# A chain of graph and expert layers on one core: the attention stage's order of work, and the number of weight buffers in two expert stages

## What is computed

```python
# L1: a shared gated layer, plus for each token its experts' second matrices
# L2: eight transformer experts, two chosen per token; keys and values of ALL tokens
def _expert(x, ...):
    q, k, v = to_heads(x @ Wqkv.T + bqkv)                 # 8 heads of 32
    attn = softmax(q * scale @ k.T)                        # over all 1354 tokens
    x = layernorm(x + (attn @ v) @ Wo.T + bo)
    h = gelu(x @ W1.T + bf1)                               # 256 -> 1024
    h = gelu(h @ W2.T + bf2)                               # 1024 -> 256
    return layernorm(x + h)
# L3: eight experts, two chosen per token
    y = layernorm(relu(x @ W1 + b1) @ W2 + b2) * gamma + beta
```

## Time and profile before

| what | value |
|---|---|
| median of 3 runs | 3437.53 us (3427.68 to 3438.13) |
| the profiled execution | 3433.94 us, its span 3432.2 us |
| routed tiles of L1 (first turned rows to last product) | 1275.7 to 1360 us of the span |
| attention stage (first to last turned unit) | 1716.8 to 2850.5 us |
| last expert stage (first weights issued to last result) | 3121.1 to 3397.8 us |
| busy, of the span | PE 73%, PE weight loads 61%, DVE 48%, ACT 32%, POOL 15% |
| mean granted TensorE clock | 0.852 |

### The profile page before, as it was taken

One profiled execution on the slowest core, in us unless ns is written; L12 is line 12 of the kernel. 1 busy time (PEld: TensorE's weight loads), 2 busy tenths in 40 slices (PEclk: granted clock), 3 DMA queues, 4 the chain that ended last, 5 costly groups with the idle time before them and its releaser, 6 DMA issues. The chain is left out here.

```text
span 3432.2 us, 53128 instructions
## 1 busy us (share of the span) xinstructions
PE 2519.3 (73%) x18781; PEld 2109.8 (61%) x18781; DVE 1643.4 (48%) x3169; ACT 1102.1 (32%) x2154; POOL 522.7 (15%) x805
## 2 busy tenths in 40 slices
PE   6978698599676687549688888888888885433334
PEld 4867597599466356438567777777777774333323
DVE  3646322322366311334377777777777774333113
ACT  2333121122133111012155555555555552231100
POOL 0000122122121015000001111111111112002112
PEclk9999699699798799769899999999999997666655
DMA  4000122243310027216634114424444201202231
GB/s 114 1 7 1 55 86 86 68 134 98 90 65 25 25 101 250 49 35 247 245 97 109 58 35 115 117 63 108 130 115 131 77 23 38 50 1 96 89 98 64
DMA packets 145018, 291.44 MB, mean 85 GB/s; under 512 B 36146, under 2 KB 73048, under 8 KB 141684
## 3 DMA queue, kind: packets, MB, share of 16 engines
q1 hardware_dynamic: 124532, 231.40, 21.9%
q0 software_dynamic: 20224, 56.65, 6.1%
HBM read 496.49 MB, written 65.74 MB: 164 GB/s over the span
## 5 line engine op out<-in xcount | busy, mean ns | idle before, releaser
L2215 PE MATMUL tx_ring<-g_ident,tx_p 128*128 128x128 f32 x2552 | 427.3, 299 | 128.6 <-issue 45.4
L2215 PEld LDWEIGHTS tx_ring<-g_ident,tx_p 128*128 128x128 f32 x2552 | 315.5, 151 | 222.9 <-issue 63.6
L2434 DVE TENSOR_REDUCE tx_neg_max<-tx_scores 128x1 f32<-128x1354 f32 x232 | 362.2, 1561 | 28.1 <-PE tx_scores L2203 28.1
L2441 DVE COPY tx_p_t<-tx_ring 128x512 f32<-128x512 f32 x464 | 306.9, 687 | 135.5 <-PE tx_ring L2215 130.1
L2341 ACT ACTIVATE tx_p<-tx_scores,tx_neg_max 128x1354 f32<-128x1354 f32 x232 | 322.3, 1389 | 77.1 <-DVE tx_neg_max L2434 76.8
L2203 PE MATMUL tx_scores<-tx_keys,tx_queries 96*128 96x512 f32 (+1 forms) x696 | 222.4, 432 | 13.7 <-DMA tx_queries<-tx_q_hi 11.3
L2348 ACT ACTIVATE tx_p_t<-tx_ring 128x384 f32<-128x384 f32 x232 | 113.4, 489 | 357.8 <-PE tx_ring L2215 356.7
L2753 PE MATMUL nee_wide<-nee_xg_t,nee_w 128*128 128x128 f32 x232 | 55.3, 414 | 156.6 <-issue 156.6
L2254 PE MATMUL tx_ring<-tx_p_t,tx_values 128*32 128x128 f32 x5104 | 151.3, 274 | 21.2 <-ACT tx_p_t L2348 20.8
L2254 PEld LDWEIGHTS tx_ring<-tx_p_t,tx_values 128*32 128x32 f32 x5104 | 135.8, 110 | 34.7 <-ACT tx_p_t L2348 34.0
L2753 PEld LDWEIGHTS nee_wide<-nee_xg_t,nee_w 128*128 128x128 f32 x232 | 48.2, 308 | 165.3 <-issue 165.3
(11 more groups left out here) (907 smaller groups left out, 5430.6 us busy)
## 6 DMA issues: line engine op xcount, KB each, us to landing
tx_keys<-expert_keys SPq DMA_DIRECT2D x696, 169.5 KB
lv1e_w<-in_L_ffn_W SPq DMA_DIRECT2D x232, 256.0 KB
tx_w<-in_L_ffn_W SPq DMA_DIRECT2D x58, 1024.0 KB
lv0e_w<-in_L_ffn_W SPq DMA_DIRECT2D x200, 256.0 KB
tx_values<-expert_values SPq DMA_DIRECT2D x58, 704.0 KB
tx_rows<-in_L_ffn_rows SPq DMA_DIRECT2D x29, 640.0 KB, 3.7
g_adj_t<-in_adj_t POOLq DMA_DIRECT2D x4, 3872.0 KB, 23.1
sro_we<-_L_ffn_expert_out_weight SPq DMA_DIRECT2D x29, 512.0 KB
```

What stands on the lines that cost most here:

```text
L2215: last = nc.tensor.transpose(ring[u % 2][:, (t - t0) * P:(t - t0 + 1) * P], p[n % 2][:, t * P:(t + 1) * P], g.ident[:])
L2434: nc.vector.tensor_reduce(neg_max[:, n % 4:n % 4 + 1], sc[n % 2][:, 0:N], AX_X, ALU.max, negate=True)\
L2441: nc.vector.tensor_copy(p_t[:, n % TURNED, t0:t0 + nt, :], ring[u % 2][:, 0:nt * P].rearrange("p (t q) -> p t q", q=P))\
```

## The change

1. Both weight rings get deeper: `ROUTED_SETS` 3 to 5, `SETS` 3 to 6. A load is then skipped only if the tile five (six) earlier had the same expert.
2. In every head PE's order becomes `turn 0, scores (head + 2), turn 1, turn 2`.
3. `second` moves from head 7 to head 6, on PE and in the ring; `add_second` moves on DVE from the end of head 7 to head 6.
4. `output` is copied out of PSUM by ACT (`keep_output`, at head 1 ahead of `keep_rows`); DVE then adds the residual in SBUF.
5. `split_queries` moves from DVE (head 2) to POOL, behind `middle_rows` and ahead of `fetch`.
6. `mix` waits for unit 2's copy only before its third group of blocks.

```diff
-ROUTED_SETS = 3
+ROUTED_SETS = 5
...
-             5: ("first0", "first1"), 7: ("second",)}
+             5: ("first0", "first1"), 6: ("second",)}
...
-                  "values0": "dve", "values1": "dve", "output": "dve", "second": "dve"}
+                  "values0": "dve", "values1": "dve", "output": "act", "second": "dve"}
...
-                for c in (1, 2):
-                    written(pe, at["heads", i, (4 * half + 3, c)])
+                written(pe, at["heads", i, (4 * half + 3, 1)])
                 for t in range(NB):
+                    if t == TG[2][0]:
+                        written(pe, at["heads", i, (4 * half + 3, 2)])
...
                         turn(i, hd, 0)
-                        turn(i, hd, 1)
                         if HEADS * i + hd + AHEAD < heads:
                             scores(HEADS * i + hd + AHEAD)
+                        turn(i, hd, 1)
                         turn(i, hd, 2)
...
-                    if hd == 7 and i:
+                    if hd == 6 and i:
                         second(i - 1)
...
+            def keep_output(i):
+                u = at["output", i, 0]
+                act.wait_ge(full, u + 1)
+                if i:
+                    act.wait_ge(x1_n_done, i)
+                nc.scalar.activation(x1[:], ring[u % 2][:, 0:D], ACT.Copy).then_inc(drained["act"], 1)
...
             def middle_stats(i):
-                u = at["output", i, 0]
-                dve.wait_ge(full, u + 1)
+                written(dve, at["output", i, 0])
                 dve.wait_ge(residual, i + 1)
-                nc.vector.tensor_tensor(x1[:], ring[u % 2][:, 0:D], x_res[:, i % 2, :], ALU.add).then_inc(drained["dve"], 1)
-                written(dve, u)
+                link(nc.vector.tensor_tensor(x1[:], x1[:], x_res[:, i % 2, :], ALU.add))
...
+            def split_queries(i):
+                written(pool, at["queries", i, 0])
+                pool.wait_ge(q_done, i + 1)
+                if i:
+                    pool.wait_ge(q_stacked, 16 * 12 * i)
+                own(nc.gpsimd.tensor_copy(q_hi[:], q[:]))
+                nc.gpsimd.tensor_tensor(q_lo[:], q[:], q_hi[:], ALU.subtract).then_inc(q_split, 1)
...
                     inverse_std(i - 1, 0, x1_seen, std1_done)
                     middle_rows(i - 1)
+                if i + 1 < tiles:
+                    split_queries(i + 1)
                 if i + 2 < tiles:
                     fetch(i + 2)
...
-SETS = 3
+SETS = 6
```

More of the change, by code:

```diff
@@ L2410, in _ @@
                         keep_inverse(i - 1, 1)
-                    if hd == 1 and i + 1 < tiles:
-                        keep_rows(i + 1)
+                    if hd == 1:
+                        if 0 < i <= tiles:
+                            keep_output(i - 1)
+                        if i + 1 < tiles:
+                            keep_rows(i + 1)
                     if hd == 2 and i + 1 < tiles:
@@ L2449, in scale_bias @@
                     .then_inc(q_scaled, 1)
[L2451 to L2457, removed]
             def inverse(i, half):
@@ L2525, in _ @@
             scale_bias(0)
-            split_queries(0)
             row_max(0)
@@ L2545, in _ @@
                             middle_norm(i - 1)
-                        if i + 1 < tiles:
-                            split_queries(i + 1)
                     if hd == 3 and i < tiles:
@@ L2551, in _ @@
                         context(i, 0)
-                    if hd == 6 and i >= 2:
-                        end_stats(i - 2)
+                    if hd == 6:
+                        if i >= 2:
+                            end_stats(i - 2)
+                        if 0 < i <= tiles:
+                            add_second(i - 1)
                     if hd == 7:
@@ L2558, in _ @@
                             inverse(i, 1)
-                        if 0 < i <= tiles:
-                            add_second(i - 1)
             back.mix(dve, spare)
@@ L2612, in _ @@
                 fetch(i)
+            split_queries(0)
             for i in range(tiles + 2):
```

## The result

The changed kernel takes 3246.3 us (median of four runs, 3244.91 to 3248.6); the kernel before took 3435.57 us (median) beside it. The ratio is 0.9453 [0.9436, 0.947]. The forecast was 3242 us. The profiled execution has a span of 3242.7 us, 189.5 us less than before's 3432.2. Where those went is read from the windows.

A forecast was written before the change was run, and what follows sets the result against it. The last expert stage was held bound by a closed chain over three weight sets, the attention stage by PE; 3434 - 165 - 30 = 3239, for the median 3242 us, range 3180 to 3325.

The forecast's parts named there:

- Part 1: Last expert stage: SETS 3 to 6 lets weight loads run ahead, paced by DMA; -165 us.
- The closed chain: Last expert stage: with three sets product, DVE, SP and transfer follow without overlap, about 11 us a round.
- I take 3.45 us, the DMA's: Last expert stage: the new pace per tile is the DMA's, 1025 KB at 297 KB per us.
- Part 2: Routed tiles: ROUTED_SETS 3 to 5 removes a 2.3 us wait, costs four more real loads; taken as 0.
- Part 3: Attention stage: waits removed, -91 us, against +63 us for the new order; taken as -30 us.
- "issue", 43.3 us: Attention stage, head 7: PE's wait for the exponent is filled by the moved `second`; all 43.3 us gone.
- the `mix` waited for unit 2's copy anyway: Attention stage, heads 0 and 4: the new order adds no wait there, so only six heads pay.
- 0.36 us more per head: Attention stage: PE idles for unit 1's bank in the new order, six heads by 29 tiles, +63 us.
- DVE `tx_p_t`, 32.5 us: Attention stage, head 3: unit 2's wait for copies behind `split_queries` goes with the split off DVE; all gone.
- The 0.36 us is larger: Rival, attention stage: all eight heads pay, port contention adds 32 us, clock falls; 3325 us, chance 0.15.
- Clock returns: Rival, attention stage: without the gap at head 7 PE runs warm; -57 us more, 3185, chance 0.2.
- The slower rival: Split on POOL becomes the bound; its pair must take 11.7 us to lose the gain; chance 0.02.

The follow-up runs named there:

- e1: The kernel before with SETS = 6 alone; 3262.97 us, ratio 0.9504.
- e5: The changed kernel with SETS = 4 instead of 6; 3298.13 us in one run.
- e10: The changed kernel with the last stage's second broadcast row not loaded after the first six tiles, same four issues per tile; 3240.63 us in one run.
- e11: e9 with a last-stage tile's two weight matrices in one buffer, loaded by one DMA, three issues instead of four; 3151.45 us, ratio 0.918.
- e12: e3 with `second` on PE and `add_second` on DVE back at head 7; 3201.96 us, ratio 0.9335.
- e3: The changed kernel with each head back to turn 0, turn 1, scores, turn 2; 3206.46 us, ratio 0.9339.
- e7: The changed kernel with DVE's two inverses between its copies of units 0 and 1 at heads 3 and 7, `end_norm` at head 6; 3191.39 us, ratio 0.9294.
- e4: The changed kernel with `split_queries` back on DVE at head 2; 3307.09 us, 61 us more than the changed kernel.
- e2: The changed kernel with both counts of weight sets back at 3, so the attention edits alone; 3425.54 us, ratio 0.9981.
- e9: The changed kernel with e7's two DVE moves and unit 1 back before the scores; 3167.15 us, ratio 0.9227.

## Why the prediction held, and which of its steps failed

**Part 1, -165 us: right in cause, short by 10, and wrong in what paces.** Measured -174.9 in the trace, -170 for e1 alone. The closed chain is shown by e5's pairs of loads. The step that failed is "I take 3.45 us, the DMA's". Its number came out, 3.46 us in the mean of 20 rounds, but the DMA engines do not set it: with an eighth of the bytes left out (e10) it was 3.49. SP's issue sets 3.2 us of it, and pauses of SP that no run explains make the rest. That the two sums agree is luck. The 10 us lie elsewhere: the first six loads, which wait for nothing, start within 13.9 us where the sum had 17.3; from the start of the 26th load to the last result it is 18.7 us instead of 22.8; and 3 us were given away in taking 165 for 168. The stage counted from its first issue is 101.8 us instead of 3230 - 3121 = 109. The step that set aside the page's rate argued from 311 GB/s. The 312 GB/s of the window above agree with it, but e10 shows that the rate did not matter. The Trainium skill ("DMA: Bandwidth & Descriptors", section on the anatomy of one DMA) has the 436 GB/s as a fit for transfers that GpSimd issues. It gave 7 us less than I took, because by it SP paces; SP does, but for another reason, and the densest 60 us read here, e11's, moved 321 GB/s. The rival "PE paces" fell: clock 0.94 in the dense part, as taken, against 0.62 over the stage before. The 26 real loads were as counted: the first skipped issue is the one at 3192.51 us.

**Part 2, 0: within the error.** The matrix wait of 2.3 us is gone, and the wait for result buffers is 2.5 us longer. No run has this edit alone.

**Part 3, -30 us: the sign right, the account wrong in four places.**

- *"issue", 43.3 us, "All gone".* The row vanished, the time did not: e12 against e3 is 4.5 us less without the edit, within the scatter. I had read what PE waits for at head 7 and named nothing that is late next. The next was DVE's queue from head 7 to head 0.
- *Head 0: "the `mix` waited for unit 2's copy anyway".* True for unit 2's copy, but unit 2 itself now waits 1.56 us for the copy of unit 0, because `row_max` comes later by the scores and DVE's `end_norm` and `inverse` stand behind it, ahead of that copy. This is the missing term; e7 prices it, with head 4's share and the clock, at 55 us.
- *"0.36 us more per head", +63 us.* The extra waits are 0.46 us. Head 1 takes 2222.38 - 2219.89 = 2.49 us from its start to the extra, where it was 2.04: 0.45 us more. As an estimate from this one head, 0.45 x 6 x 29 = 78 us; head 2's wait is shorter, 0.24 us.
- *DVE `tx_p_t`, 32.5 us, gone, and clock 0.* The split on POOL was worth 61 us in whole times and 52 us in the attention stage (e4), 15 of waits and 31 of PE's busy time among them. I had put the clock at zero between -57 and +57; it gave back 18 us of PE's busy time in the change as made.

Two terms were better than forecast: ACT `tx_h` kept 5.5 of 22.2 us where I left 14, and the wait for the bank of `output` fell from 12.6 us to 6.9 with ACT's copy, where I gained 0. That copy and the split wait of `mix` were never undone alone.

So -91 + 63 became, in the runs: about -61 for the split with its clock, about 0 for `second`, +40 for the order of the units; -21, against the 9.5 us of the trace and the 7.5 us of e2. (These prices come from different neighbours and need not add up.) That the total came out 4 us from the forecast is luck: Part 1 gave 10 us more and Part 3 some 20 us less, and 5 us came from outside both.

**The rivals.** "The 0.36 us is larger" was half right: the 0.36 was 0.45, some 15 us more by the estimate above, but the clock rose where the rival had it fall. "Clock returns" named the right price and the wrong place: the gap at head 7 went and the clock rose from 0.95 to 0.97 only, for a gap of the same length opened at head 0. With both closed (e7, e9) the clock is 1.00 and PE's busy time is 42 us below before's. The Trainium skill ("TensorE: Matmul & The Clock Gate", Part 4) says that transposes do not count as busy as matmuls do, which I took as speaking against this rival; the runs speak the other way, since e9's attention stage holds 1.00 with 396 of PE's 940 busy us in transposes (L2215). The slower rival was far off: the two POOL operations are

```profile
L2594 POOL CAST tx_q_hi<-tx_q x29: 393/398/401, 1698.2 to 2779.3; 128x256 fp32r<-128x256 f32 x29
```

```profile
L2595 POOL TENSOR_TENSOR tx_q_lo<-tx_q,tx_q_hi x29: 723/729/733, 1698.7 to 2779.8; 128x256 fp32r<-128x256 f32 x29
```

1.13 us together for the 1.5 forecast and the 11.7 that the rival needed, and the scores never had to wait for them after the first tile.

## What to carry to other kernels

A wait that is removed from one engine is time that another engine used to catch up; before it is booked as gain, add up the other engine's queue over the stretch and name what is late next, and move that work in the same edit (here worth 39 to 55 us). When a closed chain over k buffers bounds a loop, its period divided by the tiles that it serves gives the number of buffers at which the next resource takes over; here that was the issuing queue and not the bytes, though the DMA engines were 97% busy. A change of several edits can be right in sum and wrong in its parts: undoing them one at a time found one that cost 40 us and one worth nothing. And where one stage scatters by 11 us between traces of the same code, a difference of whole times below that is read stage by stage.

## What the runs showed of the hardware

**PE's longer waits and its clock.** Waits of 1.29 to 1.64 us once per tile or more (head 7 before and in e12, head 3 in e4, head 0 in after and e3) go with stage clocks of 0.95 to 0.98, and in e4 the scores behind one take 1.48 us for 0.86, most of them at 1.2 GHz. Not every such wait is followed by a slow stretch: behind the 1.56 us wait shown for after the granted clock is 1.00 from 2216 to 2222 us, and the 29 tiles of after's stage hold 15 slow stretches, e12's 10, before's 35 (the first microseconds left out). Which of the waits brings one isn't shown. Where the waits that repeat were 0.9 us at most, 123 us of waits in all in e7 and 93 in e9, the granted clock of the stage was 1.00, which is 2.4 GHz, PE's busy time was 940 us in both, and the stages differ by 28 us for 31 us of waits: there the waits cost their own length alone.

**DVE and POOL both in SBUF.** The copy that spreads the inverse over 128 columns:

```profile
L2467 DVE COPY tx_inv_rep<-tx_inv x58: 226/227/771, 1728.4 to 2838.1; 128x128 f32<-128x128 f32 x58
```

It takes 0.227 us alone and 0.77 us beside POOL's `tx_y` of 0.73 us, which began 0.04 us before it: it ends 0.08 us after POOL's, as if held until that was done. The Trainium skill's rule named in the prediction ("Advanced Engine Details and Errata", VectorE Performance Modes) agrees. The cast to the rounded type took 0.85 us in the median on DVE, where POOL worked beside it, and takes 0.40 us on POOL, so the move made the operation itself shorter.

**SP's issue.** An issue is 0.33 us in its row, but under the condition that may skip it the issues of a tile start 0.61 us apart, and 1.37 us lie between the start of a tile's last issue and of the next tile's first (after, 3141.07 to 3144.28). That makes 3.2 us for four and 2.6 us for three where nothing else holds SP, and the bytes behind them, 1025 or 897 KB, changed nothing in e10.
